# A B row and a C row for each step of a scan: one TensorE task or two

## The reference

```python
def selective_scan(u, A, Bm, Cm, Dp, dt):      # first mixer: 1024 channels, 16 states
    def step(h, xs):
        dt_t, B_t, C_t, u_t = xs
        dA = jnp.exp(dt_t[:, :, None] * A)
        dBu = dt_t[:, :, None] * B_t[:, None, :] * u_t[:, :, None]
        h = dA * h + dBu
        y = jnp.einsum('bdn,bn->bd', h, C_t)
        return (h, y)
...
# second mixer, on a context: 512 channels, 16 states
state = state * dA + (d_t * u_t)[..., None] * B_t[:, None, :]
y_t = jnp.einsum('ben,bn->be', state, C_t)
...
x = layernorm(x + mixer_1(x) with its gated feed-forward)
x = layernorm(x + mixer_2(ctx, x))
x = layernorm(x + experts(x))              # 8 experts, 2 per token, and a shared one
x = layernorm(x + segment_attention(x))    # segments of 4 tokens
x = layernorm(x + x_mixed_by_a_512_by_512_attention(ctx))
x = layernorm(x + router_bias(x))
```

## Time and profile before

| | |
|---|---|
| median of 3 runs | 3143.95 us (3140.62 to 3145.16) |
| profiled execution, its own time | 3147.43 us |
| its span in the profile | 3145.6 us |
| TensorE busy | 2488.8 us (79%) |
| VectorE busy | 2437.4 us (77%) |
| ScalarE busy | 1243.6 us |
| GpSimd busy | 1061.8 us |
| mean granted TensorE clock | 0.864 |
| last scan of a step starts | 2578.8 us |

### The profile page before, as it was taken

One profiled execution on the slowest core, in us unless ns is written; L12 is line 12 of the kernel. 1 busy time (PEld: TensorE's weight loads), 2 busy tenths in 40 slices (PEclk: granted clock), 3 DMA queues, 4 the chain that ended last, 5 costly groups with the idle time before them and its releaser, 6 DMA issues.

```text
span 3145.6 us, 20829 instructions
## 1 busy us (share of the span) xinstructions
PE 2488.8 (79%) x6508; PEld 1188.7 (38%) x6508; DVE 2437.4 (77%) x1856; ACT 1243.6 (40%) x1993; POOL 1061.8 (34%) x299
## 2 busy tenths in 40 slices
PE   4787989878959886779698876896887848969965
PEld 1234434323424443334244433342443324445532
DVE  5996898989979988899799889997998893121132
ACT  4333445544253453543534525534345332021222
POOL 1233343444424445424344454243444530000000
PEclk7886999888979998789799887897899869979986
DMA  3124436232213673022127640221265502216920
GB/s 130 35 80 151 135 109 209 80 124 80 60 34 111 201 235 123 25 101 63 37 84 226 222 138 25 87 67 40 90 198 182 164 0 87 71 44 226 294 66 14
DMA packets 160390, 350.11 MB, mean 111 GB/s; under 512 B 30680, under 2 KB 48088, under 8 KB 155608
## 3 DMA queue, kind: packets, MB, share of 16 engines
q1 hardware_dynamic: 134680, 271.89, 27.6%
q10 hardware_dynamic: 20480, 60.10, 5.1%
q0 software_dynamic: 5120, 16.78, 1.6%
HBM read 304.55 MB, written 61.73 MB: 116 GB/s over the span
## 4 chain that ended last, share of the span: by engine, by line
PE 39%; DVE 34%; issue 11%; ACT 9%; POOL 4%; DMA 3%; ACTq 0%; DVEq 0%; SPq 0%; POOLq 0%
DVE hb L1575 12%; PE ps L752 6%; PE ps L944 6%; PE ps L951 5%; DVE hb L1583 4%; DVE hb L1488 4%; PE ps L799 3%; PE ps L806 2%; POOL ya L1859 2%; PE ps L987 2%; PE ps L1078 2%; DMA ring<-in_w_edn 2%; PE ps L874 2%; PE ps L917 2%; DVE sm L1431 1%
## 5 line engine op out<-in xcount | busy, mean ns | idle before, releaser
L1859 POOL TENSOR_TENSOR ya<-ya,hb 128x2048 f32<-128x2048 f32 x188 | 857.2, 4560 | 1364.2 <-DVE hb L1575 1340.1
L1575 DVE TENSOR_TENSOR_SCAN hb<-da,hb 128x2048 f32<-128x2048 f32 x192 | 855.7, 4457 | 1.9 <-ACT da L1118 0.7
L1118 ACT ACTIVATE da<-dl,pk 128x511 f32<-128x511 f32 x768 | 489.0, 710 | 366.2 <-DVE hb L1575 359.2
L1488 DVE TENSOR_TENSOR hb<-du,ps 128x2048 f32<-128x2048 f32 x192 | 436.3, 2272 | 35.4 <-POOL ya L1859 26.2
L1583 DVE TENSOR_TENSOR hb<-hb,ps 128x2048 f32<-128x2048 f32 x192 | 437.7, 2280 | 3.6 <-PE ps L891 2.9
L799 PE MATMUL ps<-V,ring 128*128 128x512 f32 x512 | 243.6, 629 | 24.2 <-DVE V L1516 12.0
L752 PE MATMUL ps<-ring,hid 128*128 128x512 f32 x544 | 247.5, 611 | 4.2 <-DVE hid L1620 3.5
L968 PE MATMUL ps<-ring,hid 128*128 128x352 f32 x480 | 193.4, 486 | 13.1 <-DMA ring<-egu 6.9
L972 PE MATMUL ps<-ring,hid 128*128 128x352 f32 x480 | 189.5, 477 | 13.6 <-ACT X L1358 13.4
L987 PE MATMUL ps<-ring,X 128*128 128x512 f32 x360 | 186.7, 654 | 9.8 <-DMA ring<-in_w_edn 8.4
L944 PE MATMUL ps<-T,ring 128*128 128x512 f32 x352 | 170.7, 630 | 29.2 <-DVE T L1608 19.3
(11 more groups left out here) (270 smaller groups left out, 3446.0 us busy)
## 6 DMA issues: line engine op xcount, KB each, us to landing
ring<-egu SPq DMA_DIRECT2D x240, 352.0 KB, 3.9
ring<-in_w_edn SPq DMA_DIRECT2D x72, 512.0 KB, 5.3
ring<-in_w_fgu SPq DMA_DIRECT2D x44, 512.0 KB, 3.7
hid<-xrows SPq DMA_DIRECT2D x60, 256.0 KB, 4.1
yrows<-X ACTq DMA_DIRECT2D x60, 256.0 KB, 4.5
ring<-wc SPq DMA_DIRECT2D x24, 512.0 KB, 3.9
ring<-in_w_egu SPq DMA_DIRECT2D x24, 512.0 KB, 3.4
ring<-in_w_edn SPq DMA_DIRECT2D x60, 192.0 KB, 4.1
```

What stands on the lines that cost most here:

```text
L1118: i = act.activation(dav(n % 2)[:, k, 1:], dl[:, k, 1:], ACT.Exp, scale=Aneg[:, (4 * (u % 3 - 1) if u % 3 else UC) + k, m:m + 1])
L1488: dve.tensor_tensor(hbv(m % NHB), du[:, :, :], wide(ps[:, 5, :], 4), ALU.mult).then_inc(s["dbu"], 1)
L1575: dve.tensor_tensor_scan(hb[:, h, :], da[:, b % 2, :], hb[:, h, :], 0.0, ALU.mult, ALU.add)\
L1859: pool.tensor_tensor(sums, ya[:, :, :], hbv(m % NHB), ALU.add).then_inc(s["acc"], 1)
```

## The change

The single TensorE task of a step becomes two. `sa` makes only the B row of step b + 1 (and there is none for the last state of a unit), `sb` makes only the C row of step b. Each has a planned duration of 0.35 us. The planned moment was the end of the `sb` task of VectorE before; it is now 1.0 us after that end for the B row and 2.6 us after it for the C row. For the first step of a unit the B row stays 4.4 us before the planned end of `sa`, and the C row is put 2.2 us before it. The waits on semaphores are the same two as before, each now in its own task. In the plan, `sb` of VectorE waits for both tasks.

```diff
-            put(10, ("sa", n, 0), "pe", 0.65, back, (("dt_c", q, 0), "pe"), (("sa", n, 0), "dve", -4.4) if n == first else None)
+            if n < first + NST - 1:
+                put(10, ("sa", n, 0), "pe", 0.35, back + (1.0,) if n > first else back, (("dt_c", q, 0), "pe"),
+                    (("sa", n, 0), "dve", -4.4) if n == first else None)
+            put(10, ("sb", n, 0), "pe", 0.35, back + (2.6,) if n > first else back, (("dt_c", q, 0), "pe"),
+                (("sa", n, 0), "dve", -2.2) if n == first else None)
...
-            put(91, ("sb", n, 0), "dve", 4.55 if n < first + NST - 1 else 2.3, (("sa", n, 0), "dve"), (("sa", n, 0), "pe"),
-                (("sb", n - 2, 0), "pool") if n - 2 >= first else None)
+            put(91, ("sb", n, 0), "dve", 4.55 if n < first + NST - 1 else 2.3, (("sa", n, 0), "dve"), (("sb", n, 0), "pe"),
+                (("sa", n, 0), "pe") if n < first + NST - 1 else None, (("sb", n - 2, 0), "pool") if n - 2 >= first else None)
...
                     elif t == "sa":
+                        pe.wait_ge(s["dbu"], b + 1)
+                        brow(b + 1)
+                    elif t == "sb":
                         m, (se, bc) = b % NST, (selr, bcr) if b // NST % 3 else (selx, bcx)
-                        if m < NST - 1:
-                            pe.wait_ge(s["dbu"], b + 1)
-                            brow(b + 1)
                         if b:
                             pe.wait_ge(s["hc"], b)
```

## The result

| | before | after |
|---|---|---|
| median of five runs | 3140.81 us (3135.32 to 3145.16) | 3164.07 us (3158.16 to 3165.0) |
| span of the profiled execution | 3145.6 us | 3162.3 us |
| mean granted TensorE clock | 0.864 | 0.862 |

The ratio is 1.0072 [1.0059, 1.0085]: the changed kernel is about 23 us slower, where 3134 us had been forecast. The time lies above the range of 3108 to 3159 us.

What follows compares the result with a forecast made beforehand. No engine was full over the span, but VectorE nearly so before 2604 us. Terms -8.1 - 7.1 + 5.7 + 3 - 4 = -10.5 us from the 3143.95 us median gave 3134 us, range 3108 to 3159 us.

Steps and rivals of the forecast that it cites:

- Between two units: At unit ends, `dt_mm` starts ahead of the last C row, so ScalarE's chain starts earlier at three units: 8.1 us less.
- 306 to 706 us: Stretch with the chain partly on TensorE: 12.7 us of row waits freed, 8 splits cost 5.6 us; net 7.1 us less.
- Free loads: Rule that weights load ahead, making splits free and the sum 14.0 us lower; the prediction rejected it, keeping 0.70 us each.
- The first feed-forwards: Three beside scans, chain on TensorE: 4 split pairs cost 2.8 us each time, `dt_mm` returns 0.9 us; 5.7 us more.
- later rows for VectorE: Over all scan steps, rows seldom reach VectorE late: 3 us more, with 20 us as upper bound.
- The end of the last stage: Last beside-scan stage: TensorE's freed B-row waits bring the mixer's projection forward; 4 of 9 us less.
- Nothing for the rest: Elsewhere the same products and bytes, weight loads nearly in the same order: no change in time.
- The signs that were named: Right: TensorE's row waits under half of 186 us, L1556 waits 88 us; wrong: VectorE waits 20 us or more for rows.
- Split rows hold up TensorE: Rival, chance 0.23: some 40 splits where the chain is on TensorE cost 28 us; 12 us higher, 3156 us.

Runs made afterwards that it cites:

- before's, 0.15: Kernel before, planned engine latency 0.15 us; its split version moves the C row one TensorE task later at 75 steps: 3148.37 us, 1.0023.
- changed, 0.15: Changed kernel at its own planned engine latency of 0.15 us, 3164.07 us; with each C row moved directly behind its B row, 3146.02 us.
- changed, 0.14: Changed kernel with planned engine latency 0.14 us instead of 0.15: 3143.3 us; with C rows moved directly behind their B rows, 3123.34 us.
- changed, 0.16: Changed kernel with planned engine latency 0.16 us instead of 0.15: 3157.23 us; with C rows moved directly behind their B rows, 3148.06 us.
- C row late only: Changed kernel with only the C row's 2.6 us lag, B row at its old time: 3151.18 us; with pairs put together, 3132.84 us.
- pairs_together: Changed kernel's order with each C row moved directly behind its B row (75 places): 3146.02 us, 1.0028.
- pairs_in_unit_0: Changed kernel's order with C rows moved behind their B rows in the first scan unit alone (7 of 75 splits): 3153.4 us, 1.005.
- hop_016: Kernel before with planned latency between engines 0.16 instead of 0.15 us, nothing else changed: 3132.02 us, 0.998.
- b_late_only: Changed kernel with only the B row's 1.0 us lag, the C row planned without lag: 3167.89 us, 1.0097.
- changed_hop_014_pairs: Changed kernel with planned engine latency 0.14 us and C rows moved behind their B rows (76 places): 3123.34 us, 0.9951.
- hop_014: Kernel before with planned latency between engines 0.14 instead of 0.15 us, nothing else changed: 3128.77 us, 0.9963.

## Why the prediction was wrong

**What holds.** Five pairs of kernels differ only in the split pairs:

| plan | split pairs | split | together | cost of the splits |
|---|---|---|---|---|
| before's, 0.15 | 75 | 1.0023 | 1.0 | 0.23%, 7 us |
| changed, 0.15 | 75 | 1.0072 | 1.0028 | 0.44%, 14 us |
| changed, 0.14 | 76 | 1.001 | 0.9951 | 0.59%, 18 us |
| changed, 0.16 | 81 | 1.0058 | 1.0026 | 0.32%, 10 us |
| C row late only | 117 | 1.0032 | 0.9984 | 0.48%, 15 us |

All five have one sign, and in each pair of kernels all else stands in the same order on every engine. So it is shown that the C row's later place costs 7 to 18 us, 14 of the 23 us here. It is not in proportion to the number of splits: 117 cost no more than 76. The nearest two intervals, at 0.16, overlap by 0.03%.

A large part of the price seems to be paid in the first unit, where TensorE has no slack. With splits from both lags or the C row's alone, X1 came at 294 to 299 us in the five changed plans. In the five with the pairs of the first unit together it came at 282 to 290 us. The means are 11 us apart. A single X1 is good to 8 us only: `pairs_together` and `pairs_in_unit_0` run the same order up to there and had 290 and 282 us. In before's order the splits left it at 291 us, where the versions of before's plan without splits had 282 to 291 us.

With the pairs together the changed plans lie 0.28% over (0.15), 0.12% under (0.14) and 0.46% over (0.16) before's plan with the same `HOP`. This is the other part, 9 us here, and it has no sign of its own. VectorE's waits at the last states' C rows (15.7 us, and 13.0 us in the fastest plan) are in it.

**The steps, one by one.**

- *Between two units*, forecast -8.1 us. Right in its direction: alone it measured -5.0 us, and VectorE waits 83.4 us for the dt chain there instead of 96.5 us. In the changed kernel the waits fell even further, to 70.3 us. But the chain did not become shorter with them, as a task more of `xmix` stands in it, in the timeline above. At 690 us `dt_mm` was ahead of the C row too and began at 691.64 us, not at 688.2 us, because the plan had found another product for the gap.
- *306 to 706 us*, forecast -7.1 us. X1 to X3 measured -8 us, but the agreement is luck, for the mechanism failed. TensorE's waits for VectorE before rows did fall there, from 19.7 to 7.4 us. But all its waits rose, from 56.6 to 60.0 us, as the time came back before other products (before L772 from 20.4 to 30.6 us). So the 12.7 us freed did not hold other products. What fell there is VectorE's stretching beside GpSimd, 31 to 17 us. And `hop_016`, with no row moved on purpose, has 409 us there. Only 3 of this stretch's 30 pairs were split, not 8 of 22. In the first feed-forwards' units 13 were, as forecast (12), and over all steps 42%; the price of one was right too (0.70 and 0.71 us).
- *Free loads.* The rule of the Trainium skill, which says that weights are pulled ahead (TensorE: Matmul & The Clock Gate, "Step-by-step: what each phase is for"), would have made splits free. The same passage of the Trainium skill ties this to a condition, which the prediction does not weigh: the row groups must not conflict, or the load must go to the background buffer. Whether that holds at a row no run shows. The trace after agrees with the rows of before: 0.76 us idle before a row's load.
- *The first feed-forwards*, forecast +5.7 us, and *later rows for VectorE*, +3 us. Here is the other step that failed, besides the freed waits. I took a late row to be rare (0.45 us at one place) and gave 3 us for all steps; VectorE's waits for rows went from 11.9 to 32.6 us, 20.7 us more, which was the upper bound I had written down. Of these, 12.6 us stand at the last states, where the forecast let `dt_mm` pass the C row and counted nothing, and 8.0 us at split pairs. And 11.2 us of the C rows' waits lie in the stretch from 60 to 310 us, for which the sum has no term at all. I had not looked at the clock there: TensorE is full at 0.50, so a task in front of a row takes longer (eight products of a fold 1.71 us against 0.95 us, in the rows on the clock below).
- *The end of the last stage*, forecast -4 us. From X9 on the part with scans took 2 us longer. The rest after it took 6 us less, which no step foresaw; it has no rows, and its share in the plan's change stays open.
- *Nothing for the rest.* Wrong in what it left out. A new plan is a new draw: two draws that mean nothing moved the kernel by 6 and 12 us. No term and no bound held that, and a range built from the edits alone is too narrow by as much.

So the sum failed on its gains. It had 14.0 us for the splits (5.6 + 3 x 2.8), and taking them out gave 14 us; that the two are equal is partly luck, since the first is a price alone and the second is net of the waits that the late C row saves. Without the splits it had 24.5 us less, and the changed plan with its pairs together measured 9 us more. The signs that were named came out mixed: `dt_mm` went ahead and L1556 waits less, but TensorE's waits at the rows are 129.5 us and not under 93 us, and VectorE's for rows are 32.6 us, over the 20 us that was to show it wrong.

The nearest rival was *Split rows hold up TensorE*, at 0.23 and 3156 us. Its direction is right and the splits are the larger part, with two differences. It counted the price in the feed-forwards, while the first unit seems to have paid the most. And it put its time at 12 us more where the splits alone cost 14 us and the plan added 9.

**What stays open.** In the first unit two things go together in all runs, the C row's lateness for VectorE (in the profile, three of the four waits, 4.8 of 11.2 us, belong to split pairs, the fourth to the last state) and the time that splits cost TensorE while its clock is low. Over the whole run it is no clearer: in the five pairs the splits add 7.5 to 11.0 us to VectorE's waits for C rows, against costs of 7 to 18 us. `b_late_only` doesn't divide it either, as it has few splits and an order of its own. And why the changed plans' other order is worse by 9 us at 0.15 and better at 0.14 was not found. The stretching of VectorE beside GpSimd is a candidate that the traces offer (87 us in `pairs_together`, 69 us in `changed_hop_014_pairs`, by the count above), and no run tests it.

## What to carry to other kernels

An engine's idle time is not a stock to draw on: freed in one place, it came back as waits in others. Before moving work into it, ask which engine paces the loop and whether it now waits for what was freed. Where the order is planned at build time, change a meaningless constant as well and time that, before and after the change; what is smaller than this spread isn't the edit's. Small products between large ones cost 0.94 us for each visit here and 1.17 us for two in one, so keep them together.

## What the runs showed of the hardware

**The clock and the spread.** The kernel before was executed 115 times beside the experiments. In the 20 executions with a mean granted clock of 0.863 the span was 3141.8 us in the mean, in the 20 with 0.867 it was 3134.5 us. So a good part of the spread of one kernel's times goes with the clock. One place can be pointed at. `pairs_together` and `pairs_in_unit_0` issue the same order in the first unit. X1 lies 8 us apart, and the same eight products of a fold, which follow the same waits in both, ran at different clocks. In `pairs_together`:

```profile
202.65 1.71 PE L926 MATMUL ps<-R,ring 128*128 128x8 f32 x8
```

In `pairs_in_unit_0`:

```profile
196.93 0.95 PE L926 MATMUL ps<-R,ring 128*128 128x8 f32 x8
```

An order alone does not settle when the clock falls.

**VectorE beside GpSimd.** An instruction that takes 2.29 us elsewhere took nearly three times as long while GpSimd added. The timeline, after:

```profile
1764.20 4.54 POOL L1848 TENSOR_TENSOR dl<-dl,hb 128x2048 f32<-128x2048 f32 x1
1764.28 6.61 DVE L1593 SCALAR_TENSOR_TENSOR yg<-ya,yg 128x2048 f32<-128x2048 f32 x1 [6.20 <-POOL ya L1863]
```

It did its own 2.29 us of work and 4.32 us more, close to the 4.54 us of the add: it seems to have stood nearly as long as GpSimd ran. The Trainium skill says that GpSimd shares its interfaces to SBUF with VectorE and contends with instructions that have two SBUF inputs (GPSIMD Engine Reference, "1. Specifications"). This row agrees. It goes the other way too. Here the scan began first and took its usual 4.41 us, and GpSimd's instruction took 8.60 us, where 4.54 us is its time alone:

```profile
1387.10 4.41 DVE L1579 TENSOR_TENSOR_SCAN hb<-da,hb 128x2048 f32<-128x2048 f32 x1
...
1387.25 8.60 POOL L1823 TENSOR_TENSOR X<-X,V 128x2048 f32<-128x2048 f32 x1 [8.84 <-DVE V L1606]
```

In these rows the instruction that began first ran at its own pace and the other stood. Over the whole trace VectorE's stretching grew from 76.2 us (before) to 86.5 us (after) by the count above, most of VectorE's 15.1 us of added busy time. Its total alone doesn't decide the result: the fast `hop_014` has 85 us of it.
